# Six idle-time products on TensorE at the end of a gated scan, and GpSimd's splits of the second weight block behind a later wait

## The chip, the cores and the metric

The kernel runs on one core of one Trainium2 chip. Its time is the device time of one execution in microseconds (us). The core's engines are TensorE (PE in the rows; PEld is its weight load), VectorE (DVE), ScalarE (ACT), GpSimd (POOL) and SyncE (SP), which here only issues transfers. Each runs its own instructions in the order in which they are written, and they wait for one another through semaphores.

## The reference

Four layers stand in series, each added to its input and followed by a LayerNorm: an mLSTM attention layer, a mixture of 16 experts with the best 4 of each token, a gated linear attention (GLA) layer and a mixture of 32 experts with the best 8. There are 4 x 256 = 1024 tokens of 256 values in float32. The change lies between the end of the third layer and the start of the fourth:

```python
def step(S, inp):                      # GLA: 16 heads, 8 keys and 16 values each
    qt, kt, vt, gt = inp
    S = S * jnp.exp(gt)[..., None] + kt[..., None] * vt[..., None, :]
    ot = jnp.einsum('bhk,bhkv->bhv', qt, S)
    return (S, ot)
...
mu = o.mean(-1, keepdims=True)
var = ((o - mu) ** 2).mean(-1, keepdims=True)
o = (o - mu) * jax.lax.rsqrt(var + EPS)
o = o.transpose(0, 2, 1, 3).reshape(B, L, D)
return jax.nn.silu(gproj) * o @ Wo.T
...
logits = x @ gate_weight.T             # last layer: 32 experts
probs = jax.nn.softmax(logits.astype(jnp.float32), axis=-1).astype(logits.dtype)
topv, topi = jax.lax.top_k(probs, TOP_K)
...
gu = x @ w_gu.T
g, u = jnp.split(gu, 2, axis=-1)
h = jax.nn.silu(g) * u
acc = acc + h @ w_d.T * c_e[:, None]
```

## The kernel before, in words

**Precision.** Products of float32 values are done as three faster products: each operand is split into a rounded high part and the remainder, the low part, and `mm3` (its products are all put down to L1970) adds high x high, low x high and high x low. So each activation that goes into a product is first copied rounded out of PSUM by ScalarE (`XH`) and then subtracted by VectorE (`XL`); the latter counts up `lo_done` once for a pair of 128-token tiles. There are 8 tiles (`NT`), so each of the four LayerNorms' or head outputs' turnings brings `lo_done` up by 4: to 12 when the input of the GLA output projection is split (L1549), and to 16 when the input of the dense expert layer is (L1588). Weights are split by GpSimd: `high` (L811) rounds, `low` (L816) subtracts.

**The GLA scan.** The 16 value columns v are gone through one after another. TensorE's `spread(v)` (L2495) copies the values over the keys' rows, VectorE multiplies by the keys (L1904) and scans over the tokens (L1923), GpSimd multiplies the state by the queries (L824), and TensorE's `gather_o(v)` (L2507) sums over the keys with a 0/1 matrix of 32 columns. For the last v, GpSimd does half of the product (the 128x512 L824) and VectorE the other half. Between its steps GpSimd splits block 0 of the last layer's weights. ScalarE then copies and squares the outputs (L1251, L1252), TensorE sums the squares of each head (`sum_squares(k)`, L2547, once for each half of the values), VectorE makes the head's scale (L1355, L1356) and applies gate and scale (L1943, L1378) tile by tile, TensorE turns the tiles (L2225), ScalarE and VectorE split them, and TensorE does the output projection.

**The LayerNorm by halves.** `layernorm_by_halves` does tiles 0 to 3, then 4 to 7. VectorE takes the statistics (L1559, L1567), adds the small constant (L1569, 128x4) and inverts (L1570); ScalarE takes the root (L1010), VectorE makes the bias (L1576), and both normalise two tiles each (L1579, L1013). TensorE turns them (L2247), ScalarE makes the high part (L1019), VectorE the low part (L1588).

**The dense expert layer.** All 32 experts are computed for all tokens, in 8 blocks ("quads") of 4 experts. A block has 6 steps: 2 halves of the tokens x 3 chunks of 128 hidden values, 48 steps in all. `gate_up(i)` is 12 products (step 0's are L2290 and L2295). ScalarE applies SiLU to the gate (L1047) and, in the first `AHEAD` = 6 steps, copies the up part (L1052), and GpSimd multiplies the two (L880, `mixed_pool`). From step 6 on VectorE does that product (L1677). ScalarE's SiLU of step i waits for the product of step i - 2, and TensorE's step i waits for SiLU and copy of step i - 2, whose PSUM bank it takes. The down products run `LAG` = 10 steps behind.

**The router** runs beside steps 0 to 5. TensorE makes the logits (`route_half`, L2256) and turns them (L2264); VectorE does the rest in one chain of some 30 small instructions, each waiting for the one before: L1607 to L1611, the exponential on ScalarE (L1034), the eight largest (L1614), the rules (L1616 to L1652), and the combine weights `CW` (L1654 to L1665). Behind step 5 TensorE turns `CW` (`turn_weights`, L2328); it waits for it there, and what is behind it on TensorE waits, too. The turned weights are spread over rows and multiplied into the hidden values by GpSimd (L889).

**GpSimd's order** around the change is: the query products of the scan, with block 0's splits between them; the four splits of block 1 (gate/up high 128x1536 and low, down high 128x768 and low), today behind `lo_done` of 12; the six products of L880; then the splits of the later blocks between the L889. SyncE's transfers of block 3 wait for the splits of block 1 (`gate_split`, `down_split`), and the combine weights' transfer stands behind them.

`keep_warm(n, b)` writes n products of a zero matrix, 128 rows x 512 columns in bf16, into PSUM bank b; nobody reads them. It is there already at two places, 18 at the start (bank 7) and 2 behind the output projection (bank 0).

Of the kernel before, what the change touches and what calls it, by code (L numbers as in the profile page):

```python
# [28 lines left out]
def build_kernel(nc, a, out):  # L29
# [3 lines left out]
    NT = T // P  # L33
# [11 lines left out]
    DV1 = D // NH1  # L45
# [17 lines left out]
    with ExitStack() as ctx:  # L63
# [3 lines left out]
        def sem(name):  # L67
            return ctx.enter_context(nc.semaphore(name))
# [3 lines left out]
        def bank(n):  # L72
            return PS[:, n, :]
# [265 lines left out]
        lo_done = sem("lo_done")  # L339
# [147 lines left out]
        def quad_slot(q):  # L487

            n, c = GCOLS, DCOLS  # L490
            if q % 2 == 0:
                return [flat(EG[:])[:, 0:n], EW4[:, 0:n], EW4[:, n:2 * n],
                        flat(ED[:])[:, 0:c], EW4[:, 2 * n:2 * n + c], EW4[:, 2 * n + c:2 * n + 2 * c]]
            return [FA[:, 0:n], RA[:, 0:n], RA[:, n:2 * n],
                    FA[:, GLA_WORDS:GLA_WORDS + c], RA[:, 2 * n:2 * n + c], flat(W1H[:])[:, 0:c]]
# [52 lines left out]
        def _(sp):  # L548
# [15 lines left out]
            def load_expert(e, par):  # L564

                land_g, _, _, land_d, _, _ = MOE.slot(par)
                sp.dma_start(land_g.rearrange("p (k c) -> p k c", k=KD),
                             a["gateup0"][bass.ds(e, 1)].rearrange("o (k p) i -> p (o k) i", p=P)
                             ).then_inc(ld_exp[par], 16)
                sp.dma_start(land_d.rearrange("p (c d) -> p c d", d=D),  # L570
                             a["down0"][bass.ds(e, 1)].rearrange("o (c p) d -> p (o c) d", p=MOE.IP)
                             ).then_inc(ld_exp[par], 16)
# [68 lines left out]
        def _(pool):  # L641
# [195 lines left out]
                    low(dl, d, dh, whole, d_rounded).then_inc(down_split, 1)  # L837

            g, gh, gl, d, dh, dl = quad_slot(1)
            pool.wait_ge(lo_done, 3 * (NT // 2))  # L840
            pool.wait_ge(gate_ld[1], 32 * KD)
            g_rounded = high(gh, g, whole)
            low(gl, g, gh, whole, g_rounded).then_inc(gate_split, 1)
# [4 lines left out]
            def next_split(i):  # L848

                at, j = divmod(i, 2 * CHUNKS)
                q = at + 1
                if 2 <= q < QUADS:
                    g, gh, gl, _, _, _ = quad_slot(q)
                    if j == 0:
                        pool.wait_ge(gate_up_mm, 2 * 2 * CHUNKS * (q - 1))
                        pool.wait_ge(gate_ld[q % 2], 32 * KD * (q // 2 + 1))
                        rounded["g0"] = high(gh, g, half(0))
                    if j == 2:
                        low(gl, g, gh, half(0), rounded["g0"])  # L860
                    if j == 3:
                        rounded["g1"] = high(gh, g, half(1))
                    if j == 4:
                        low(gl, g, gh, half(1), rounded["g1"]).then_inc(gate_split, 1)
                q = at - 1
                if 2 <= q < QUADS:
                    _, _, _, d, dh, dl = quad_slot(q)
                    if j == 0:
                        pool.wait_ge(dn_done, 2 * CHUNKS * (q - 1))
                        pool.wait_ge(down_ld[q % 2], 16 * (q // 2 + 1))  # L870
                        rounded["d"] = high(dh, d, whole)
                    if j == 1:
                        low(dl, d, dh, whole, rounded["d"]).then_inc(down_split, 1)

            rounded = {}
            for i in range(STEPS + LAG - 1):
# [5 lines left out]
                v = i - (LAG - 1)  # L882
# [1080 lines left out]
        def _(pe):  # L1963
# [25 lines left out]
            def keep_warm(n, b):  # L1989

                for _ in range(n):
                    pe.matmul(bank(b), zb[:, 0:P], zb[:], start=True, stop=True, skip_group_check=True)
# [275 lines left out]
            def residual(src, tiles=range(NT)):  # L2268

                for t in tiles:  # L2270
                    pe.matmul(bank(4 + t // 2)[:, (t % 2) * D:(t % 2 + 1) * D], ident[:], src[:, t, :],
                              start=(t % 2 == 0), stop=True, skip_group_check=True)
# [6 lines left out]
            def moe_pe():  # L2279

                def gate_up_first():

                    b = step_bank(0)
                    _, gh, gl, _, _, _ = quad_slot(0)
                    pe.wait_ge(gate_split, 1)
                    pe.wait_ge(hi_done, 3 * (NT // 2) + 2)
                    for up in range(2):
                        for k, (xh, _) in enumerate(xm(0)):
                            for j, g in enumerate((gh, gl)):
                                pe.matmul(bank(b + up), chunk_of(g, k, up, 0), xh, start=(k == 0 and j == 0), stop=False,  # L2290
                                          skip_group_check=True)
                    pe.wait_ge(lo_done, 3 * (NT // 2) + 2)
                    for up in range(2):
                        for k, (_, xl) in enumerate(xm(0)):
                            ins = pe.matmul(bank(b + up), chunk_of(gh, k, up, 0), xl, start=False, stop=(k == KD - 1),  # L2295
                                            skip_group_check=True)
                        ins.then_inc(gate_up_mm, 1)
# [190 lines left out]
            def spread(v):  # L2488

                s = v % 2  # L2490
                if v >= 2:
                    pe.wait_ge(s_done, v - 1)
                for hf in range(2):
                    for i, part in enumerate((VTH, VTL)):
                        ins = pe.matmul(bank(2 * s + hf), rep1[:, v % 8, :], part[:, v // 8, hf * BANK:(hf + 1) * BANK],  # L2495
                                        start=(i == 0), stop=(i == 1))
                ins.then_inc(vr_mm, 1)

            def gather_o(v):

                pe.wait_ge(qs_done, v + 1)
                if v == DV1 - 1:
                    pe.wait_ge(qs_last, 1)
                for hf in range(2):

                    q = (32 * ((v % 8) // 2) + 64 * hf) % P
                    ins = pe.matmul(bank(4 + 2 * (v // 8) + hf)[q:q + 32, :], block2[:, v % 2, :],  # L2507
                                    QS[:, v % 2, hf * BANK:(hf + 1) * BANK], start=(v % 2 == 0), stop=(v % 2 == 1))
                ins.then_inc(qs_used, 1)
# [14 lines left out]
            def output_gate(t):  # L2524

                p = t // 2
                if t == 0:
                    pe.wait_ge(vt_lo, 4)
                    pe.wait_ge(w_split, 5)
                if t % 2 == 0 and p >= 2:  # L2530
                    pe.wait_ge(og_silu, p - 1)
                b = bank(6 + p % 2)
                mm3(b[:, (t % 2) * D:(t % 2 + 1) * D], xs(t), ws(W1H, W1L, G1, D), t % 2 == 0, True)
                if t % 2:
                    for part in (BGH, BGL):
                        ins = pe.matmul(b, rep1[0:1, 0, 0:1].broadcast_to([1, P]),
                                        part.unsqueeze(1).broadcast_to([1, 2, D]), start=False, stop=True,
                                        skip_group_check=True)
                    ins.then_inc(og_mm, 1)

            def sum_squares(k):

                pe.wait_ge(osq_act, 2 + k)
                for t in range(NT):
                    if k == 1 and t == NT // 2:
                        pe.wait_ge(osq_dve, 1)
                    ins = pe.matmul(bank(5)[:, t * NH1:(t + 1) * NH1], OSQ[k][:, t * P:(t + 1) * P], head_sum,  # L2547
                                    start=(k == 0 and t == 0), stop=(k == 1), skip_group_check=True)
                if k == 1:
                    ins.then_inc(osq_sum, 1)  # L2550
# [6 lines left out]
            for v in range(DV1):  # L2557
                if v + 2 < DV1:
                    if v + 2 == DV1 // 2:
                        pe.wait_ge(vt_lo, 4)  # L2560
                    spread(v + 2)
                for t in gate_tiles.get(v, ()):
                    output_gate(t)
                if v == SQUARES_AT:
                    sum_squares(0)
                if v == SQUARES_AT + 1:
                    residual(XA, (0, 1))
                if v == DV1 // 2:
                    pe.wait_ge(og_silu, NT // 2)
                gather_o(v)  # L2570
            sum_squares(1)

            pe.wait_ge(ot_evac, 3)
# [106 lines left out]
```

## Time and profile before

| | |
|---|---|
| median of 3 executions | 591.24 us (590.7 to 593.32) |
| the profiled execution, its own time | 589.8 us |
| its span | 588.0 us |
| TensorE busy (matmul) | 523.6 us, 89% of the span |
| GpSimd busy | 348.8 us, 59% |
| VectorE busy | 327.0 us, 56% |
| ScalarE busy | 230.5 us, 39% |
| chain that ended last, by engine | PE 61%, DVE 14%, DMA 5%, issue 5%, POOL 4%, ACT 2% |

All positions are us from the start of the span. In a row of the timeline stand the start, the length, the engine, the line of the kernel, the operation, output<-input and how many instructions the row merges; brackets at its end tell for how long the engine had been idle and what released it.
### The profile page before, as it was taken

What the parts mean: (1) busy time and instruction counts of PE and PEld (TensorE: products, weight loads), DVE (VectorE), ACT (ScalarE), POOL (GpSimd) and SP (SyncE); (2) the same over time, 40 slices, a digit from 0 to 9 for tenths busy, and PEclk for the clock granted to TensorE, in tenths of its full rate; (3) what the DMA queues carried; (4) which work ended last, traced back from release to release, by engine and by line L of the source; (5) the groups of instructions that cost most, each with busy time, mean ns of one, the idle gap of its engine ahead of it and who ended that gap; (6) DMA issues with size and microseconds to landing.
All of it is one profiled execution on the core that took longest, in us unless ns stands there. A gap on an engine that the chain in (4) does not pass through costs nothing.

```text
span 588.0 us, 9553 instructions
## 1 busy us (share of the span) xinstructions
PE 523.6 (89%) x3033; PEld 426.0 (72%) x3035; DVE 327.0 (56%) x726; ACT 230.5 (39%) x539; POOL 348.8 (59%) x316
## 2 busy tenths in 40 slices
PE   7999986339998999988989768999999999999994
PEld 4766666329887989966645438778888888888884
DVE  4635688634666444435998958563333252433276
ACT  3555542315554766545502022663232323232334
POOL 3394012777998797671377824254947657698180
PEclk9979998759998999999989968899999999999999
DMA  8999983245675766543000050204234343144022
GB/s 249 365 386 386 349 296 132 101 137 173 201 245 175 208 188 180 172 124 107 1 1 1 0 161 3 80 10 141 74 107 121 114 143 99 36 135 140 5 72 71
DMA packets 72864, 83.69 MB, mean 142 GB/s; under 512 B 7617, under 2 KB 63698, under 8 KB 72818
## 3 DMA queue, kind: packets, MB, share of 16 engines
q1 hardware_dynamic: 33490, 38.90, 22.0%
q10 hardware_dynamic: 35968, 35.26, 17.9%
q0 software_dynamic: 3360, 8.93, 4.9%
q8 instruction: 26, 0.43, 0.3%
q14 instruction: 20, 0.16, 0.1%
HBM read 48.61 MB, written 34.47 MB: 141 GB/s over the span
## 4 chain that ended last, share of the span: by engine, by line
PE 61%; DVE 14%; DMA 5%; issue 5%; POOL 4%; ACT 2%; ACTq 0%; DVEq 0%; POOLq 0%
PE PS L1970 47%; DMA FA<-xg 4%; POOL xg L708 3%; DVE FA L1923 2%; DVE PS L1904 2%; PE PS L2376 2%; PE PS L2495 2%; PE PS L2045 1%; PE PS L2067 1%; PE PS L2400 1%; PE PS L2507 1%; DVE HC L1378 1%; DMA FA<-yg,tix 1%; POOL FA L783 1%; PE PS L2192 1%
## 5 line engine op out<-in xcount | busy, mean ns | idle before, releaser
L1970 PE MATMUL PS<-XH,EW 128*128 128x512 f32 x392 | 129.8, 395 | 0.2 <-DVE EW L1278 0.2
L1677 DVE TENSOR_TENSOR FA<-OGATE,PS 128x512 f32<-128x512 f32 x42 | 28.9, 688 | 108.8 <-ACT OGATE L1047 90.7
L1970 PEld LDWEIGHTS PS<-XH,EW 128*128 128x128 f32 x392 | 73.7, 188 | 16.3 <-DVE EW L1278 0.7
L1970 PE MATMUL PS<-EW,XH 128*128 (+2 forms) x252 | 77.0, 389 | 3.6 <-issue 2.2
L1047 ACT ACTIVATE OGATE<-PS 128x512 f32<-128x512 f32 x48 | 28.7, 599 | 124.1 <-PE PS L1970 124.1
L1970 PE MATMUL PS<-XL,EW 128*128 128x512 f32 x196 | 77.0, 393 | 0.0
L1970 PE MATMUL PS<-EW 128*128 128x256 f32 x288 | 63.2, 284 | 0.6 <-DVE W1L L1682 0.4
L824 POOL TENSOR_TENSOR FA<-FA,QT 128x1024 f32<-128x1024 f32 (+1 forms) x16 | 37.4, 2338 | 32.5 <-DVE FA L1923 32.5
L1970 PE MATMUL PS<-EW,W1L 128*128 128x256 f32 x192 | 54.3, 283 | 0.0
L1970 PEld LDWEIGHTS PS<-EW 128*128 128x128 f32 x288 | 49.1, 189 | 4.2 <-DVE W1L L1682 1.5
L1970 PEld LDWEIGHTS PS<-EW,XH 128*128 128x128 f32 x252 | 44.8, 198 | 8.3 <-issue 2.8
L1682 DVE TENSOR_TENSOR W1L<-FA,EW 128x512 fp32r<-128x512 f32 x48 | 46.6, 978 | 2.8 <-ACT EW L1070 2.8
L1970 PE MATMUL PS<-EW,XL 128*128 (+2 forms) x126 | 46.6, 370 | 0.0
L889 POOL TENSOR_TENSOR FA<-FA,HC 128x512 f32<-128x512 f32 x24 | 34.5, 1442 | 16.7 <-DMA HC<-cw_room 16.7
L708 POOL DMA_INDIRECT xg<-XB,tix x32 | 31.3, 978 | 19.4 <-DVE tix L1463 10.4
L889 POOL TENSOR_TENSOR FA<-FA,QT 128x512 f32<-128x512 f32 x24 | 34.2, 1433 | 14.2 <-DMA QT<-cw_room 14.2
L1970 PEld LDWEIGHTS PS<-XL,EW 128*128 128x128 f32 x196 | 37.0, 189 | 6.8
L1970 PE MATMUL PS<-EW,EHH 112*128 x188 | 40.2, 306 | 0.1
L1923 DVE TENSOR_TENSOR_SCAN FA<-FA,PS 128x1024 f32<-128x1024 f32 x16 | 36.6, 2286 | 0.5
L1782 DVE TENSOR_TENSOR XL<-PS,XH 128x256 fp32r<-128x256 f32 x47 | 19.9, 424 | 30.0 <-ACT XH L1114 29.7
L1793 DVE TENSOR_TENSOR SQ<-SIL,PS 128x224 f32<-128x224 f32 x47 | 18.2, 388 | 32.7 <-ACT SIL L1133 32.2
L1970 PEld LDWEIGHTS PS<-EW,W1L 128*128 128x128 f32 x192 | 36.3, 189 | 0.0
(395 smaller groups left out, 1210.7 us busy)
## 6 DMA issues: line engine op xcount, KB each, us to landing
xg<-EQ ACTq DMA_DIRECT2D x1, 16384.0 KB, 60.7
EG<-in_gateup SPq DMA_DIRECT2D x16, 448.0 KB, 4.0
yg<-EQ ACTq DMA_DIRECT2D x1, 6016.0 KB, 19.7
FA<-xg ACTq DMA_DIRECT2D x47, 128.0 KB, 2.2
yg<-FA ACTq DMA_DIRECT2D x47, 128.0 KB, 2.6
ED<-in_down SPq DMA_DIRECT2D x16, 224.0 KB, 4.5
EG<-in_gateup SPq DMA_DIRECT2D x16, 192.0 KB, 3.0
FA<-in_gateup SPq DMA_DIRECT2D x16, 192.0 KB, 3.2
```

The costliest lines, as they stand in the source:

```text
L708: pool.indirect_dma_start(out=xg, out_offset=bass.IndirectOffsetOnAxis(ap=slots[:, n:n + 1], axis=0), in_=XB[:, t, :], in_offset=None).the ...
L824: pool.tensor_tensor(QS[:, v % 2, c], STATE[:, v % 2, c], QT[:, c], ALU.mult).then_inc(qs_done, 1)
L889: pool.tensor_tensor(mixed[:, v % MIXED, :], mixed[:, v % MIXED, :], spread_w[v % SPREADS], ALU.mult).then_inc(weighted, 1)
L1047: act.activation(sil_t[:, i % 2, :], bank(b), ACT.Silu).then_inc(sil_done, 1)
L1677: dve.tensor_tensor(mixed[:, i % MIXED, :], sil_t[:, i % 2, :], bank(step_bank(i) + 1), ALU.mult).then_inc(mixed_dve, 1)
L1682: dve.tensor_tensor(h_lo[:, v % TURNED, :], mixed[:, v % MIXED, :], h_hi[:, v % TURNED, :].bitcast(F32), ALU.subtract).then_inc(h_lo_done, 1)
L1782: dve.tensor_tensor(XL[:, :, c], bank(2 + i % 2)[:, 0:D].rearrange("p (k c) -> p k c", k=KD), XH[:, :, c].bitcast(F32), ALU.subtract).then ...
L1793: dve.tensor_tensor(HH[:, i % 2, 0:I], SIL[:, i % 2, 0:I], bank(i % 2)[:, I:2 * I], ALU.mult).then_inc(sh_ready, 1)
L1904: dve.tensor_tensor(spread_v(v), KT, spread_v(v), ALU.mult).then_inc(d1_done, 1)
L1923: dve.tensor_tensor_scan(STATE[:, v % 2, :], DEC, spread_v(v), 0.0, ALU.mult, ALU.add).then_inc(s_done, 1)
L1970: ins = pe.matmul(o, l, r, start=start and i == 0, stop=stop and i == n - 1, skip_group_check=True)
L2376: ins = pe.transpose(bank(2 + i % 2)[:, k * P:(k + 1) * P], XG[:, i % 4, k * P:(k + 1) * P], ident[:])
```

## The change

On GpSimd, the splits of block 1 wait for `lo_done` of 16 in place of 12. On TensorE, four `keep_warm` products come ahead of the last gathering (v = 15) and two behind it, into bank 0, which the last even-numbered v has left.

```diff
@@ -837,7 +837,7 @@
                     low(dl, d, dh, whole, d_rounded).then_inc(down_split, 1)
 
             g, gh, gl, d, dh, dl = quad_slot(1)
-            pool.wait_ge(lo_done, 3 * (NT // 2))
+            pool.wait_ge(lo_done, 4 * (NT // 2))
             pool.wait_ge(gate_ld[1], 32 * KD)
             g_rounded = high(gh, g, whole)
             low(gl, g, gh, whole, g_rounded).then_inc(gate_split, 1)
@@ -2567,7 +2567,10 @@
                     residual(XA, (0, 1))
                 if v == DV1 // 2:
                     pe.wait_ge(og_silu, NT // 2)
+                if v == DV1 - 1:
+                    keep_warm(4, 0)
                 gather_o(v)
+            keep_warm(2, 0)
             sum_squares(1)
 
             pe.wait_ge(ot_evac, 3)
```

TensorE's instructions around the last gathering (L2507; FA holds the query products, block is the 0/1 matrix, zb the zero matrix), before against after, with the semaphores waited for:

```order
 L2507 MATMUL PS<-FA,block 32x512 [waits qs_done]
 L2507 MATMUL PS<-FA,block 32x512
+L1992 MATMUL PS<-zb 128x512 x4
 L2507 MATMUL PS<-FA,block 32x512 [waits qs_last,qs_done]
 L2507 MATMUL PS<-FA,block 32x512
+L1992 MATMUL PS<-zb 128x512 x2
 L2547 MATMUL PS<-sums,FA 128x16 [waits osq_act]
 L2547 MATMUL PS<-sums,FA 128x16 x3
 L2547 MATMUL PS<-sums,FA 128x16 [waits osq_dve]
```

The four stand ahead of the wait for the last query product, the two ahead of the wait for the squares. The wait that changes on GpSimd has the same semaphore and another number, so its order of instructions is the same before and after.

## Rows read from the trace of the kernel before

**Rows 1.** Stretches: length, busy time of each engine, PEclk, DMA share, GB/s.

```profile
342.92:356.57 13.65, 10.92 (x46) 9.19 (x47) 6.98 (x18) 4.00 (x7) 1.49 (x1) 0.50 0.57 173
...
370.22:373.64 3.42, 3.42 (x9) 2.63 (x8) 2.01 (x10) 2.13 (x4) 0.00 (x0) 0.50 0.40 125
```

**Rows 2.** Timeline of TensorE around the last gathering.

```profile
333.27 1.85 PE L2547 MATMUL PS<-sums,SQ 128*128 128x16 f32 x16
...
341.53 1.05 PE L2507 MATMUL PS<-FA,block 128*32 128x512 f32 x4 [2.37 <-POOL FA L824]
...
344.46 1.92 PE L2507 MATMUL PS<-FA,block 128*32 128x512 f32 x4 [1.88 <-POOL FA L824]
...
347.57 3.60 PE L2547 MATMUL PS<-sums,FA 128*128 128x16 f32 x16 [1.19 <-ACT FA L1252]
```

**Rows 3.** Timeline of GpSimd and VectorE in the LayerNorm.

```profile
360.89 1.48 POOL L811 TENSOR_SCALAR EW<-FA 128x1536 fp32r<-128x1536 f32 x1 [16.48 <-DVE XL L1549]
...
362.46 3.49 POOL L816 TENSOR_TENSOR EW<-FA,EW 128x1536 fp32r<-128x1536 f32 x1
...
363.88 2.09 DVE L1569 TENSOR_SCALAR rv<-mv 128x4 f32<-128x4 f32 x1
...
366.46 0.30 DVE L1576 SCALAR_TENSOR_TENSOR nb<-mv,rstd 128x4 f32<-128x4 f32 x1 [0.27 <-ACT rstd L1010]
...
366.83 1.81 POOL L816 TENSOR_TENSOR W1H<-FA,EW 128x768 fp32r<-128x768 f32 x1
...
370.84 0.17 DVE L1569 TENSOR_SCALAR rv<-mv 128x4 f32<-128x4 f32 x1
```

**Rows 4.** ScalarE and VectorE split the dense layer's input; chain of waits, TensorE.

```profile
374.75 1.09 ACT L1019 ACTIVATE XH<-PS 128x512 fp32r<-128x512 f32 x2 [0.52 <-PE PS L2247]
...
375.39 1.42 DVE L1588 TENSOR_TENSOR XL<-PS,XH 128x256 fp32r<-128x256 f32 x4 [2.82 <-ACT XH L1019]
...
392.91 7.20 PE PS L1970 x31
```

**Rows 5.** Timeline of VectorE in the router.

```profile
380.48 0.69 DVE L1607 TENSOR_REDUCE LG<-PS 128x256 f32<-128x512 f32 x1 [3.67 <-PE PS L2264]
...
381.66 0.84 DVE L1611 TENSOR_TENSOR LG<-LG,rsum 128x256 f32<-128x256 f32 x1
...
385.65 1.31 DVE L1637 TENSOR_TENSOR t<-t,rsum 128x64 f32<-128x64 f32 x1
...
387.50 0.88 DVE L1642 SCALAR_TENSOR_TENSOR rbest<-rsum,rbest 128x8 f32<-128x8 f32 x1
...
388.68 0.23 DVE L1645 SCALAR_TENSOR_TENSOR t<-t 128x64 f32<-128x64 f32 x1
...
389.50 0.16 DVE L1657 SCALAR_TENSOR_TENSOR rsum<-rv,rsum 128x8 f32<-128x8 f32 x1
...
391.39 0.42 DVE L1665 TENSOR_TENSOR CW<-CW,rsum 128x256 f32<-128x256 f32 x1
```

**Rows 6.** Timeline of GpSimd beside the router.

```profile
379.66 2.56 POOL L880 TENSOR_TENSOR FA<-OGATE 128x512 f32<-128x512 f32 x2 [11.01 <-ACT OGATE L1052]
...
385.58 1.29 POOL L880 TENSOR_TENSOR FA<-OGATE 128x512 f32<-128x512 f32 x1 [3.36 <-ACT OGATE L1052]
...
387.07 1.29 POOL L880 TENSOR_TENSOR FA<-OGATE 128x512 f32<-128x512 f32 x1 [0.21 <-ACT OGATE L1052]
```

**Rows 7.** Timeline of GpSimd and VectorE in the sparse layer.

```profile
160.27 0.94 POOL L750 TENSOR_SCALAR EW<-EG 128x896 fp32r<-128x896 f32 x1
...
160.32 0.93 DVE L1631 TENSOR_TENSOR t<-t,rsum 128x32 f32<-128x32 f32 x1
```

**Rows 8.** Stretches around an earlier gap (columns as in rows 1); timeline of TensorE.

```profile
295.13:298.55 3.42, 1.56 (x7) 0.21 (x5) 3.42 (x4) 0.00 (x0) 1.85 (x1) 1.00 0.00 0
...
298.55:301.96 3.41, 3.01 (x10) 2.63 (x11) 3.38 (x3) 0.00 (x0) 2.99 (x2) 0.50 0.00 0
...
391.87 1.05 PE L2328 MATMUL PS<-ident,CW 128*32 128x128 f32 x8
```

## The prediction

> **What bounds the kernel now.** I read the granted clock by stretch first, then the stretch around the last gathering on TensorE, then VectorE against GpSimd from 360 to 392 us, and last the chain of waits. The clock shows two low stretches here: half speed (1.2 of 2.4 GHz) from 342.92 to 356.57 us and again from 370.22 to 373.64 [rows 1]. Before the first fall TensorE had done one 1.05 us gathering and then waited for GpSimd [rows 2]. What it does at half speed is on the path: the last gathering takes 1.92 us where the one before it took 1.05, and the second sum of squares takes 3.60 us where the first took 1.85 [rows 2]. Behind them come VectorE's head statistics and gating, the output projection, the LayerNorm, and the dense expert layer, where products follow one another, 31 in 7.20 us or 0.232 us each, twelve to a step, 2.8 us [rows 4]. It has to stop once there: the turning of the combine weights (L2328, start 391.87) needs the router's result from VectorE, whose last instruction (L1665) ends at 391.81 [rows 5, 8]. Today the two arrive nearly together.
>
> **The six products.** Four stand between the gatherings of v = 14 and v = 15, where TensorE is idle for 1.88 us, two between the last gathering and the sum of squares, where it is idle for 1.19 us [rows 2]. A product of 512 columns takes 0.23 us at full clock [rows 4], which I double for half clock. Four are 0.9 to 1.9 us against 1.88 of idle time, two are 0.5 to 0.9 against 1.19. So they cost nothing themselves; without that cover they would cost at most 2.8 us. If they hold the clock, the last gathering gives back 1.92 - 1.05 = 0.87 us and the sum of squares 3.60 - 1.85 = 1.75, together **-2.6 us**. Bounds: 0 (the clock falls all the same) and -2.6; behind the sum the slow transposes lie beside VectorE's gating, so I count nothing for them. I take -2.6, since the idle time behind the gathering of v = 14 falls from 1.88 + 1.19 to about 1.7 us, in two pieces.
>
> **The wait on GpSimd, in the LayerNorm.** `lo_done` reaches 12 when VectorE has done the low parts for the output projection; GpSimd begins the second block's splits there, at 360.89 us [rows 3]. They hold VectorE up: the tiny L1569 (128x4) takes 2.09 us and ends at 365.97, just as GpSimd's L816 ends (362.46 + 3.49 = 365.95); its second instance, with GpSimd idle, takes 0.17. The next two-operand instruction, L1576 (0.30 us), ends with the next split, too, and may give back 0.15 more [rows 3]. With the splits gone from here that is 1.92 + 0.15 = **-2.1 us**, on the path, since TensorE stands still for the normalised tiles. Bounds: -1.9 and -2.1. The SyncE queue is not late for it: it loads block 3 after `gate_split` reaches 2, now some 11 us later, but still ahead of its next wait, the combine weights.
>
> **The wait on GpSimd, in the router.** This is where I think the gain goes. `lo_done` reaches 16 with the last L1588, which ends at 375.39 + 1.42 = 376.81 [rows 4]. After the change it ends some 5.2 us earlier, at 371.6: 2.6 + 2.1, and 0.5 more, if the second low stretch goes with the shorter gap (L1019 was held until 374.75 by TensorE's slow products [rows 4]). GpSimd's four splits fill 360.89 to 366.83 + 1.81 = 368.64, 7.75 us [rows 3], so they now run from 371.6 to 379.4. The six products of gate and up (L880) queued behind them take 1.29 us each. The first two ran at 379.66 to 382.22 [rows 6]; the first now runs at 379.4 as before, although all else is 5 us earlier. From there GpSimd is never idle for long: products at 379.4, 380.7, 382.2, 383.6, 385.0, with 0.2 us let in for VectorE between two of them. The last waits for TensorE: step 4 needs the SiLU of step 2, which waits for the first product (380.7 + 0.5), and steps 4 and 5 take 2 x 2.8 us, so to 386.8; its operand is copied by 387.3 and it ends at 388.5.
> VectorE's router starts with L1607, at 380.48 before [rows 5]; by 2.6 + 2.1 and 1.2 for the low clock stretch, it starts at 374.6. Its chain from L1607 to the end of L1665 is 11.33 us, of which 2.2 are waiting today: L1611 takes 0.84 where a like instruction (L1665) takes 0.42, L1637 1.31 where L1645 takes 0.23, L1642 0.88 [rows 5]. L1637 and L1642 end within 0.1 us of a GpSimd product's end (386.87 and 388.36) [rows 5, 6]. Now GpSimd runs all through it. L1611 waits for the long split (to 376.7), L1620 for the last one, and L1623, L1635, L1637, L1639, L1642 each for one of the products, about 1 us each. The sixth product then catches L1645 or L1657. From its end at 388.5 the rest is 391.81 - 388.68 = 3.1 us or 391.81 - 389.50 = 2.3 [rows 5], so the weights are ready at 390.8 to 391.6, against 391.81 before. I take 391.3, **-0.5 us for everything up to here**: 5.4 of the 5.9 us that the router starts earlier are waited away. Bounds: no waits beyond today's, 385.9; every one of eleven two-operand instructions caught by a product, 392.6.
> The rows show single waits with idle GpSimd around them; that VectorE loses a whole GpSimd instruction at each of its two-operand instructions is shown by L1631, too, 0.93 us for 128x32, ended as L750 ends (160.27 + 0.94) [rows 7]. The Trainium skill (SBUF — State Buffer, "Who interferes with whom") speaks against this change here: a VectorE instruction with two SBUF inputs shares a read port with GpSimd, and the second to issue is blocked for the whole of the first. By that rule the router's chain waits as above and the sum is my forecast; by today's rows alone, three waits in the chain, the sum would be the first rival. The trace agrees with the rule for L1637 (1.31 us) and does not show back-to-back products against a chain.
>
> **The clock behind the new gap.** TensorE would end step 5 at 386.8 and stand still until 391.3, 4.5 us. Before, there is no such gap. After 295.13 to 298.55, with 1.56 us of work in 3.42, the next stretch was granted 0.50 although TensorE was busy 3.01 us in it [rows 8]; in 370.22 to 373.64 a stretch full of products at half speed lost 1.7 us [rows 1]. So returning work loses 0 (the low stretch lies within the gap) to 1.7 us, or 2.5 if the rise is late; I take **+1.6**, near the row of 370.22, since TensorE's work behind the gap is all on the path.
>
> **Sum.** -0.5 + 1.6 = +1.1 us against the profiled execution's 589.8, that is 590.9. The median shown is 591.24, 1.4 above that execution, so I forecast **592.3 us**. A measurement here tells about 0.5% from no change, 3 us: below 588.3 is faster, above 594.2 slower.
>
> **Rivals.**
> 1. **The router isn't held up.** If VectorE gets its turn between the products at no cost, the weights are there at 385.9 and TensorE, which the first product of GpSimd still holds until step 5 ends at 386.8, turns them at once: 386.8 - 391.8 = -5.0 us, 586.2. For it: today's VectorE reductions and PSUM readers don't wait. Against it: L1637, L1642, L1569 and L1631 did [rows 3, 5, 7].
> 2. **Half of the waits.** Some router instructions slip between products, the weights come at (385.9 + 391.3) / 2 = 388.6, 3.2 us earlier than before, the gap is under 2 us and the clock holds: 588.0.
> 3. **Slower: the clock falls at the last gathering all the same.** Then -2.6 is lost, everything from the sum of squares on is 2.6 us later with the router's waits unchanged: +1.1 + 2.6 = +3.7, 594.9. It decides if four products don't suffice before 342.92: the fall came 0.34 us after the gathering's end (342.58) [rows 1, 2], so only that much of the new work lies ahead of it, if the chip decides at the same moment.
> 4. **The products don't do what they are for, and the wait does nothing either** (splits and products move, the clock too): within 1 us, 591.2.
>
> **How the numbers follow.** Forecast (589.5 to 593.8) 0.50; rival 1 0.10; rival 2 0.15, half of it under 588.3; rival 3 0.17, most of it above 594.2; rival 4 0.08. Faster by over 0.5%: 0.10 + 0.08 = 0.18, to which I add 0.02 for a forecast with less of a gap: 0.20. Slower by over 0.5%: 0.15 from rival 3 and 0.02 from the forecast with every wait at its upper bound: 0.17. The same: 0.63. The range reaches from a little under rival 2 to rival 3: 587.2 to 594.9; the forecast's own is 589.5 to 593.8.
>
> **What would show it.** Right: the last gathering near 1.05 us and the sum of squares near 1.85, the granted clock 1.00 there; L1569 0.17; the splits starting as the last L1588 ends; L1623 to L1642 near 1.2 us each, ending with an L880; TensorE idle 3 to 5 us in front of L2328, released by L1665, and the clock low behind it. Wrong: L2328 starting within 0.5 us of step 5's end (rival 1), or L2547 still at 3.6 us (rival 3).

## The result, and the profile after

The changed kernel takes 593.09 us (median of 20 executions, 587.08 to 599.46), the kernel before, measured beside it, 589.49 (20 executions, 584.18 to 596.59). The ratio is 1.0062, with an interval of 1.0038 to 1.0087: 0.6% slower, 2.2 to 5.1 us. Ratios, here and below, leave out executions more than 1.5% above the fastest of the same kernel. The level before is 1.75 us lower than in the first three executions, so the forecast of 592.3 lies closer to the measured time than its step of +1.1 us does to the measured +3.6.

In the profiled execution (span 592.8 us) the gathering of v = 14 starts at 344.58, 3.05 us later than before [rows 2]; nothing ahead of it was changed. So positions are compared from that start on: the turning of the combine weights (L2328) comes 50.30 us behind it, before 391.87 - 341.53 = 50.34. Up to there nothing is won. I call this distance M, the time from the start of L2328 to the end of the span R (before 588.0 - 391.87 = 196.1, after 592.8 - 394.88 = 197.9), and the two together L: 246.5 before, 248.2 after.

TensorE around the last gathering, in the timeline of the changed kernel:

```profile
344.58 1.05 PE L2507 MATMUL PS<-FA,block 128*32 128x512 f32 x4 [2.37 <-POOL FA L824]
345.79 0.81 PE L1992 MATMUL PS<-zb 128*128 128x512 bf16 x3 [0.16 <-issue]
347.51 1.05 PE L2507 MATMUL PS<-FA,block 128*32 128x512 f32 x4 [0.91 <-POOL FA L824]
348.50 0.60 PE L1992 MATMUL PS<-zb 128*128 128x512 bf16 x2
349.75 1.96 PE L2547 MATMUL PS<-sums,FA 128*128 128x16 f32 x16 [0.65 <-ACT FA L1252]
```

They answer to [rows 2]. The last gathering takes 1.05 in place of 1.92 us, the sum of squares 1.96 in place of 3.60, and the new products lie in the idle time. This part went as forecast: -2.5 us.

The granted clock in the same profile, by stretch (length, busy time of PE, PEld, DVE, ACT and POOL, PEclk, DMA share, GB/s), against [rows 1]:

```profile
342.00:357.00 15.00, 9.59 (x63) 6.02 (x62) 10.81 (x22) 5.16 (x9) 4.17 (x2) 1.00 0.54 159
357.00:361.00 4.00, 3.15 (x13) 2.60 (x13) 3.90 (x13) 1.23 (x3) 0.00 (x0) 0.57 0.00 1
361.00:394.90 33.90, 28.52 (x156) 22.53 (x156) 24.32 (x82) 18.73 (x35) 16.64 (x12) 1.00 0.12 36
394.90:398.80 3.90, 3.90 (x15) 3.04 (x16) 0.68 (x1) 0.59 (x1) 1.59 (x1) 0.56 0.14 33
```

The long low stretch has gone, but a short one stands at 357 to 361, on the way into the output projection, and one at 395 to 399, behind L2328. The low stretch in the dense layer's first step has gone, too.

GpSimd and VectorE in the LayerNorm and ahead of the router, against [rows 3, 4]:

```profile
365.44 0.17 DVE L1569 TENSOR_SCALAR rv<-mv 128x4 f32<-128x4 f32 x1
374.25 1.42 DVE L1588 TENSOR_TENSOR XL<-PS,XH 128x256 fp32r<-128x256 f32 x4 [2.18 <-ACT XH L1019]
375.76 1.48 POOL L811 TENSOR_SCALAR EW<-FA 128x1536 fp32r<-128x1536 f32 x1 [28.31 <-DVE XL L1588]
377.32 3.49 POOL L816 TENSOR_TENSOR EW<-FA,EW 128x1536 fp32r<-128x1536 f32 x1
380.78 1.01 POOL L811 TENSOR_SCALAR EW<-FA 128x768 fp32r<-128x768 f32 x1
381.87 1.84 POOL L816 TENSOR_TENSOR W1H<-FA,EW 128x768 fp32r<-128x768 f32 x1
383.67 3.90 POOL L880 TENSOR_TENSOR FA<-OGATE 128x512 f32<-128x512 f32 x3
387.77 1.29 POOL L880 TENSOR_TENSOR FA<-OGATE 128x512 f32<-128x512 f32 x1 [0.20 <-ACT OGATE L1052]
```

L1569 has its 0.17 us, and the splits start 0.1 us behind the last L1588. They fill GpSimd until 383.7, where the first products (L880) begin, three of them without a break.

VectorE's router in the same timeline, against [rows 5]:

```profile
378.94 0.69 DVE L1607 TENSOR_REDUCE LG<-PS 128x256 f32<-128x512 f32 x1 [3.27 <-PE PS L2264]
...
380.12 0.97 DVE L1611 TENSOR_TENSOR LG<-LG,rsum 128x256 f32<-128x256 f32 x1
...
383.03 0.70 DVE L1620 SCALAR_TENSOR_TENSOR rv<-rsum,rbest 128x8 f32<-128x8 f32 x1
...
384.00 1.03 DVE L1623 TENSOR_TENSOR t<-top,rsum 128x64 f32<-128x64 f32 x1
385.07 1.19 DVE L1635 TENSOR_TENSOR t<-t,alpha 128x64 f32<-128x64 f32 x1
386.30 0.22 DVE L1636 TENSOR_REDUCE rsum<-t 128x8 f32<-128x64 f32 x1
386.55 1.10 DVE L1637 TENSOR_TENSOR t<-t,rsum 128x64 f32<-128x64 f32 x1
...
389.65 1.26 DVE L1647 TENSOR_TENSOR t<-top,t 128x64 f32<-128x64 f32 x1
...
392.62 1.24 DVE L1663 SCALAR_TENSOR_TENSOR CW<-HC,PR 128x256 f32<-128x256 f32 x1
393.90 0.93 DVE L1665 TENSOR_TENSOR CW<-CW,rsum 128x256 f32<-128x256 f32 x1
```

The chain from L1607 to the end of L1665 takes 15.89 us against 11.33. Nine instructions wait now (L1642, at 0.89, is the ninth), all with two operands in SBUF; before it was three (L1611, L1637 and L1642). Between them L1636, a reduction, takes its 0.22 us with GpSimd busy. TensorE pays for it in front of L2328:

```profile
394.88 1.83 PE L2328 MATMUL PS<-ident,CW 128*32 128x128 f32 x8 [3.33 <-DVE CW L1665]
```

It stands still for 3.33 us, and L2328 takes 1.83 us at the low clock in place of 1.05.

### The profile page after: what moved, and what is told of

The parts are those of the page before. It is cut to its first block, busy times and chain, and to the rows that moved or that the text cites. A ratio compares the mean times of both kernels' runs of the same rounds, so it can differ in the third digit from the quotient of the medians.

```text
span 592.8 us, 9564 instructions
## 1 busy us (share of the span) xinstructions
PE 525.8 (89%) x3038; PEld 424.4 (72%) x3041; DVE 330.7 (56%) x726; ACT 230.2 (39%) x539; POOL 348.6 (59%) x316
## 4 chain that ended last, share of the span: by engine, by line
PE 60%; DVE 13%; POOL 6%; DMA 6%; issue 5%; ACT 2%; ACTq 0%; POOLq 0%; DVEq 0%
PE PS L1970 46%; DMA FA<-xg 3%; POOL xg L708 3%; DVE FA L1923 2%; POOL FA L783 2%; DMA FA<-yg,tix 2%; DVE PS L1904 2%; PE PS L2067 2%; PE PS L2045 2%; PE PS L2376 2%; PE PS L2495 1%; PE PS L2400 1%; PE PS L2507 1%; DVE HC L1378 1%; PE PS L2030 1%
## 5 line engine op out<-in xcount | busy, mean ns | idle before, releaser
L1970 PE MATMUL PS<-XH,EW 128*128 128x512 f32 x392 | 131.3, 398 | 1.2 <-ACT OGATE L1047 1.0
L1970 PEld LDWEIGHTS PS<-EW 128*128 128x128 f32 x288 | 49.3, 190 | 4.3 <-DVE W1L L1682 1.5
L1970 PE MATMUL PS<-EW,XL 128*128 (+2 forms) x126 | 46.6, 370 | 0.0
L811 POOL TENSOR_SCALAR EW<-FA 128x768 fp32r<-128x768 f32 (+1 forms) x11 | 11.2, 1027 | 51.2 <-DVE XL L1588 28.3
```

The lines of the kernel that those rows point to most:

```text
L1970: ins = pe.matmul(o, l, r, start=start and i == 0, stop=stop and i == n - 1, skip_group_check=True)
```

## The experiments

Three groups of four kernels ran, each beside the kernel before, whose medians were 630.06 us (17 executions), 630.75 (23) and 589.90 (29). In the profiles of the first two groups, from two different chips, the part ahead of the gathering of v = 14 takes 37 to 53 us longer than in the first profile of before. The third group ran on the chip of the second and does not show this, so it isn't the chip; what it is stays open. The four ratios of the first group rest on two executions of before (624.06 and 615.14 us) and stand above the ratios of the medians, so they decide nothing, and I read M, R and L from the profiles there.

| kernel | M | R | L | L1607 to L1665 | gap at L2328 |
|---|---|---|---|---|---|
| before | 50.3 | 196.1 | 246.5 | 11.3 | none |
| before_again | 49.3 | 196.2 | 245.4 | 11.3 | none |
| changed | 50.3 | 197.9 | 248.2 | 15.9 | 3.33 |
| after_again | 50.2 | 199.2 | 249.3 | 15.9 | 3.33 |
| wait_only | 51.8 | 198.0 | 249.8 | 15.9 | 3.34 |
| products_only | 46.8 | 196.4 | 243.2 | 11.3 | none |
| parted (three profiles) | 45.0, 45.8, 45.0 | 196.2, 196.4, 196.2 | 241.1, 242.2, 241.2 | 11.6 | 0.3 |
| parted_only | 46.6 | 196.4 | 243.0 | 11.6 | 0.33 |
| warm_gap | 49.3 | 196.2 | 245.5 | 15.9 | filled |
| no_splits | 45.6 | 196.4 | 242.0 | 11.3 | none |
| two_only | 49.3 | 199.1 | 248.4 | 15.9 | 3.34 |
| four_only | 49.3 | 197.9 | 247.2 | 15.9 | 3.33 |

The kernel before once more (before_again, no edit) had a median of 589.48 us against 589.90 (0.9999, 0.9964 to 1.0035). Expected were L of 245.5 to 247.5 us, a last gathering of 1.9 and a sum of squares of 3.0 to 3.6; they were 245.4, just under, 1.92 and 3.60.

**How M adds up.** The profiles of one placement of the splits differ by a few parts only, and M can be worked out from these: a last gathering at half speed adds 0.87 us (1.92 - 1.05), a sum of squares at half speed 1.64 (3.60 - 1.96). Products_only has neither, 46.77; with both added that is 49.28, and before_again has 49.26. The changed kernel without either is 49.28 (two_only, four_only, warm_gap); with the slow gathering it is 50.15, as after_again has, and with both 51.79, where wait_only has 51.82. The parted splits without either are 44.97; with the slow sum 46.61, and parted_only has 46.59; with the slow gathering 45.84, as parted_again has. So moving the splits costs 2.5 us of M, as much as the products win where the last gathering keeps the clock, and parting them wins 1.8. The first profile of before has 1.1 us more than before_again. Those come from its second low stretch, 370.22 to 373.64 [rows 1], which before_again doesn't have: there the clock is 1.00 from 363 us to L2328.

The sum of squares took 1.96 us in all ten profiles with products and 3.60 in all four without. The last gathering is another matter: it took 1.92 us in three of the ten (after_again, parted_again, no_splits), and 1.05 in parted_only, which has no products there.

**Each half alone.** The products without the new wait:

```diff
-            pool.wait_ge(lo_done, 4 * (NT // 2))
+            pool.wait_ge(lo_done, 3 * (NT // 2))
```

> The changed kernel with the splits' wait put back to lo_done of 12: the six products alone. Measure M is the time from the start of the gathering of v = 14 (L2507) to the start of the turning of the combine weights (L2328): 50.34 us in the profile before, 50.30 in the changed kernel. Theory (the products hold the clock and are worth 2.5 us; the router's waits come from the moved splits): last gathering 1.05 us, sum of squares near 1.9, L1569 still near 2.1, L1607 to the end of L1665 near 11.3 us, M 46.5 to 47.9, TensorE idle under 1 us at L2328, time 2.5 to 3.8 us under before (ratio 0.9935 to 0.9958). Rival (the clock falls elsewhere instead and takes the gain back): M 49.5 to 50.5, ratio 0.999 to 1.001.

Median 626.14 us against 630.06 (ratio 1.0125, 0.9989 to 1.0261). M is 46.77, L 2.2 to 3.3 us under the two profiles of before. L1569 still waits:

```profile
400.13 2.08 DVE L1569 TENSOR_SCALAR rv<-mv 128x4 f32<-128x4 f32 x1
```

The wait without the products, which is the kernel before with 4 in place of 3:

> The kernel before with the splits' wait at lo_done of 16, without the six products. Theory: L1569 0.17 us, L1607 to the end of L1665 15 to 16.5 us, TensorE idle 3 to 4.5 us in front of L2328 and the clock low behind it for up to 3.5 us; the last gathering 1.9 and the sum of squares 3.6 us; M 52.3 to 53.1, time 3.8 to 4.8 us over before (ratio 1.0065 to 1.008). Rival (the wait alone gains by the freed L1569, and the changed kernel lost its time elsewhere): M 48 to 49, ratio 0.996 to 0.999.

Median 632.26 (1.0241, 1.0088 to 1.0394). M is 51.82, half a microsecond under the expected range; the chain (15.9 us) and the gap are as expected.

```profile
384.86 3.60 PE L2547 MATMUL PS<-sums,FA 128*128 128x16 f32 x16 [1.19 <-ACT FA L1252]
...
430.64 1.05 PE L2328 MATMUL PS<-ident,CW 128*32 128x128 f32 x8 [3.34 <-DVE CW L1665]
```

The gap is the same 3.34 us, although the products are missing and everything ahead of it lies elsewhere: the wait makes the gap by itself. The wait is the half that costs, 3.3 to 4.4 us of L against the two profiles of before; the products gain.

**The gap filled.**

```diff
-                    pe.wait_ge(cw_step, CW_READY)
                     pe.wait_ge(sil_done, AHEAD - 1)
                     pe.wait_ge(up_copied, AHEAD - 1)
+                    keep_warm(14, 2)
+                    pe.wait_ge(cw_step, CW_READY)
```

> The changed kernel with 14 more of the unread bf16 products behind step 5 of the dense layer, in the gap in front of L2328. Theory (the low clock behind the gap costs 1.9 us): M 50.0 to 50.6 as in the changed kernel, L2328 near 1.05 us, granted clock 1.00 behind it, from the start of L2328 to the end of the span 196.1 us as in the profile before against 197.9 in the changed kernel; ratio to before 0.999 to 1.002. Rival (the gap's low stretch costs nothing that isn't hidden): 197.9 us stays, ratio 1.003 to 1.008.

Median 632.65 against 630.06 (1.0193, 1.007 to 1.0315), which tells nothing between the two theories; its profile does. R is 196.2 as before, against 197.9 with the gap:

```profile
443.00:447.00 4.00, 3.99 (x22) 3.33 (x23) 0.73 (x2) 1.19 (x2) 1.64 (x1) 1.00 0.15 33
```

The clock is 1.00 behind L2328, so the low stretch behind the gap costs 1.7 us. The splits, and with them the transfers of block 3, are as late here as in the changed kernel, so their lateness costs nothing. In after_again and two_only the low stretch is longer and costs 2.9 us; both profiles are of long executions, 645.99 and 642.85 us. In after_again:

```profile
444.57:451.04 6.47, 5.99 (x19) 4.59 (x20) 1.10 (x2) 1.18 (x2) 2.01 (x2) 0.51 0.13 27
```

M, 49.29, is 0.7 us under what I expected: no low stretch fell into it here. In time it isn't shown that filling the gap wins anything.

**The changed kernel once more.**

> The changed kernel once more, on the chip of this group. M (start of the gathering of v = 14 to start of L2328) 49.2 to 50.4 us, the part from there to the end of the span 197.5 to 198.1, L1607 to the end of L1665 15.5 to 16.2, gap in front of L2328 over 3 us: all as on the first chip, if these are the program's own and not the chip's. Rival: they differ by more than 1 us from profile to profile, and the sum over these parts says nothing.

Median 631.99 against 630.75 (1.0014, 0.9972 to 1.0057): in this group the changed kernel isn't shown to be slower. M and the chain repeat, R doesn't (199.2 for 197.5 to 198.1). And the clock fell in the midst of the four products:

```profile
395.88 1.47 PE L1992 MATMUL PS<-zb 128*128 128x512 bf16 x4
397.83 1.92 PE L2507 MATMUL PS<-FA,block 128*32 128x512 f32 x4 [0.48 <-POOL FA L824]
399.68 0.62 PE L1992 MATMUL PS<-zb 128*128 128x512 bf16 x2
400.93 1.96 PE L2547 MATMUL PS<-sums,FA 128*128 128x16 f32 x16 [0.63 <-ACT FA L1252]
```

It is back before the sum of squares. The products don't always keep the clock up; what the profiles show is that the low stretch behind them is short. A low stretch of about 4 us also lies 7 to 12 us behind the start of the gathering of v = 14 in eight of the ten profiles with products, where it adds nothing to M. In the first profile of the changed kernel it comes at 357 us, 12.4 behind, and adds 1.0 (50.30 against 49.28); warm_gap has none.

**Two or four of the six.** Each kernel is the changed one without the other `keep_warm`.

> The changed kernel without the four products ahead of the last gathering, the two behind it kept. Theory (the four keep the clock from falling behind the gathering of v = 14): last gathering 1.9 us, sum of squares 3.0 to 3.6, M 51.5 to 53. Rival (the two suffice): gathering 1.05 to 1.9 and sum of squares under 2.2, M 49 to 50.5.

> The changed kernel with the four products ahead of the last gathering and without the two behind it. Theory (what counts is that the clock is back, or has not fallen, when the sum of squares starts; the four alone do that): sum of squares under 2.1 us, gathering 1.05 or 1.92, M 49.2 to 50.6. Rival (the two are what brings the clock back): sum of squares 3.0 to 3.6, M 51 to 53.

Gathering 1.05 and sum of squares 1.96 us in both, M 49.27 and 49.28; as single executions they took 642.85 us (before 630.75 in its group) and 590.96 (before 589.90). For two_only that is the rival's reading, but one profile doesn't show that the two suffice: in it a low stretch had ended 9.5 us ahead of the gathering of v = 14, as in parted_only, whose last gathering takes 1.05 us without any product, so this may be luck. What each of the six is worth stays open.

**Without the splits.**

```diff
-            g_rounded = high(gh, g, whole)
-            low(gl, g, gh, whole, g_rounded).then_inc(gate_split, 1)
+            one = lambda w: w[:, 0:2]
+            g_rounded = high(gh, g, one)
+            low(gl, g, gh, one, g_rounded).then_inc(gate_split, 1)
...
-            d_rounded = high(dh, d, whole)
-            low(dl, d, dh, whole, d_rounded).then_inc(down_split, 1)
+            d_rounded = high(dh, d, one)
+            low(dl, d, dh, one, d_rounded).then_inc(down_split, 1)
```

> The changed kernel with the four splits of block 1 cut to 2 columns each, waits and counts unchanged: most of block 1's high and low parts isn't computed. Theory (the splits, which still run when the router starts, delay the products of GpSimd and by them the router and TensorE): first L880 soon after the SiLU of step 0, L1607 to the end of L1665 11.0 to 12.0 us, no gap over 1 us in front of L2328, M 44.5 to 46. Rival (L880's six products alone hold the router up as long): L1607 to L1665 14 us or more, M 48 or more.

One execution, 625.31 us. The timeline of GpSimd (lines behind the edit are 1 higher):

```profile
412.99 0.20 POOL L816 TENSOR_TENSOR W1H<-FA,EW 128x2 fp32r<-128x2 f32 x1
414.64 2.56 POOL L881 TENSOR_TENSOR FA<-OGATE 128x512 f32<-128x512 f32 x2 [1.46 <-ACT OGATE L1053]
420.56 1.29 POOL L881 TENSOR_TENSOR FA<-OGATE 128x512 f32<-128x512 f32 x1 [3.37 <-ACT OGATE L1053]
```

With the same wait and no work behind it, the products keep the breaks that they have in [rows 6], the chain is back at 11.33 us and the gap is gone. What held the router up is the splits' 7.8 us of GpSimd, directly and by pushing the products together.

**Parted splits.** The products stay, the splits begin early again, and the three behind the first wait until VectorE is past the instructions that stalled (L1569, L1576):

```diff
-            pool.wait_ge(lo_done, 4 * (NT // 2))
+            pool.wait_ge(lo_done, 3 * (NT // 2))
             pool.wait_ge(gate_ld[1], 32 * KD)
             g_rounded = high(gh, g, whole)
+            pool.wait_ge(ln_bias, LN_BASE[2] + 1)
             low(gl, g, gh, whole, g_rounded).then_inc(gate_split, 1)
+            pool.wait_ge(ln_bias, LN_BASE[2] + 2)
             pool.wait_ge(down_ld[1], 16)
```

> The changed kernel with the splits begun at lo_done of 12 again, but parted: the rounding of the gate block first, its long low part only after the bias of the first half's LayerNorm (ln_bias, L1576), the down block after that of the second half. Theory (what costs is only which VectorE instruction lies beside which split): L1569 0.17 us twice, the splits done before the first GpSimd product, L1607 to the end of L1665 11 to 12 us, no gap over 1 us in front of L2328, M 44.7 to 46.0, time 4.3 to 5.6 us under before (ratio 0.9905 to 0.993). Rival (the low parts then hold up the second half's instructions, L1569 and L1588, and the gain is given back): M 46.5 to 48, ratio 0.994 to 0.998.

> The parted splits once more, beside the changed kernel. M 44.5 to 45.5 and 196.0 to 196.4 us behind it as in its first run; time 1.2 to 1.5% under the changed kernel and 0.8 to 1.1% under the kernel before. Rival: the gain is the chip's of the first group, under 0.5%.

> The kernel with products and parted splits, a third time. M 44.7 to 46.0, 196.0 to 196.5 us behind it, L 241 to 242.3; time 0.7 to 1.0% under before. Rival: the median differs from before by less than 0.5%.

Medians 624.21 against 630.06 (1.0081, 0.9994 to 1.0169), 624.80 against 630.75 (0.9915, 0.9828 to 1.0001) and 585.30 against 589.90 (0.9938, 0.9905 to 0.9971): 4.6 to 6.0 us less. M of the second, 45.84, is over its range, since the last gathering took 1.92 us there; L1569 is 0.17 twice in all three. GpSimd in the third profile (lines behind the edit are 2 higher, so L1571 is L1569 and L1578 is L1576):

```profile
356.87 1.48 POOL L811 TENSOR_SCALAR EW<-FA 128x1536 fp32r<-128x1536 f32 x1 [13.97 <-DVE XL L1551]
360.80 3.46 POOL L816 TENSOR_TENSOR EW<-FA,EW 128x1536 fp32r<-128x1536 f32 x1 [2.45 <-DVE nb L1578]
365.72 0.83 POOL L811 TENSOR_SCALAR EW<-FA 128x768 fp32r<-128x768 f32 x1 [1.46 <-DVE nb L1578]
366.64 1.83 POOL L816 TENSOR_TENSOR W1H<-FA,EW 128x768 fp32r<-128x768 f32 x1
```

and VectorE beside it:

```profile
359.90 0.17 DVE L1571 TENSOR_SCALAR rv<-mv 128x4 f32<-128x4 f32 x1
```

The long split lies between the two halves' biases, the last ends at 368.5, well ahead of the router. Both stalls are avoided. By the interval of the third group this kernel is 0.3 to 1.0% faster than the one before; the second group's interval just reaches 1. Its median is the lowest in each of the three groups.

**The same without the products.**

> The kernel before with the parted splits and without the six products. Theory (parting is worth 1.9 us in the LayerNorm, the products 1 to 2.6, and the two add up): L (start of the gathering of v = 14 to the end of the span) 243.5 to 245.0, last gathering 1.9, sum of squares 3.0 to 3.6, L1569 0.17, time 1.9 to 2.5 us under before (ratio 0.996 to 0.997). Rival (only the splits mattered): L 241 to 242.5 as with the products.

Median 587.15 (0.9924, 0.9892 to 0.9957), last gathering 1.05 us, sum of squares 3.60:

```profile
343.95 1.05 PE L2509 MATMUL PS<-FA,block 128*32 128x512 f32 x4 [1.87 <-POOL FA L824]
346.19 3.60 PE L2549 MATMUL PS<-sums,FA 128*128 128x16 f32 x16 [1.19 <-ACT FA L1254]
```

L is 242.97, half a microsecond under the expected range and 0.8 to 1.9 over the three with products. The medians agree (1.85 us), but the ratios stand the other way round (0.9938 with products, 0.9924 without) and their intervals overlap: that the products add to the parting is shown by the profiles, not by the times.

## Why the prediction was right and where it was off

**The way was right.** The mechanism, the place where the gain goes and the sign of the first comparison held: the LayerNorm's stall went, the router's chain lengthened by 4.6 us, a gap opened in front of L2328, and the clock fell behind it.

**The size was not.** I forecast +1.1 us and held 0.63 for "the same"; measured is +3.6 (2.2 to 5.1), past my bound of 3 us, a case I gave 0.17. L says +1.7 to +3.9 from profile to profile, and after_again +0.1% (-0.3 to +0.6), so how much slower the kernel is stays uncertain. Term by term:

- **The products, -2.6.** Here they gave -2.5 at their place, but the clock fell again at 357, which took 1.0 back: the last L2225 took 1.09 us there against 0.63, and L2271 1.59 against 1.03. Comparing L with and without them: products_only -2.2 to -3.3 against before, the changed kernel -0.5 to -1.6 against wait_only, parted -0.8 to -1.9 against parted_only. I took the upper bound of the term; the mean of these seven differences is -1.7. This term was the most mis-sized.
- **The LayerNorm, -2.1.** L1569 went from 2.09 to 0.17 in each kernel that moved the long split away, L1576 from 0.30 to 0.16. I spoke of L1576 as the next two-operand instruction, but L1569 isn't one: its row reads one tile (rv<-mv), and it had the longest stall.
- **The router.** I had the splits begin 30.1 us behind the gathering of v = 14; they begin at 31.2 (375.76 - 344.58). I had L1607 at 33.1; it is at 34.4. Of the 5.9 us that I moved it ahead, 1.2 were for the low stretch at 370.22, which before_again doesn't have, so that part was there to be won in one of the two profiles of before only. The chain was forecast at 16.7 and is 15.9. L2328 was to start at 49.8 and starts at 50.3. The waits fell on the instructions that I named up to L1642, but for L1639 (0.23 us), and at the end on L1647, L1663 and L1665, since the last product came later, and the next block's split behind it.
- **The clock behind the gap, +1.6.** 1.7 us by warm_gap and four_only, 2.9 by the long executions of after_again and two_only. The gap was forecast at 4.5 and is 3.3, with another 1.0 us between steps 3 and 4.

With -1.7 for the first term and 1.7 for the last the sum is +2.1, just under the measured interval; with 2.9 for the last it is +3.3, inside it. **Rival 1** falls by the chain of 15.9 us in six profiles. **Rival 3** is half true: in after_again the clock did fall at the last gathering, but it was back before the sum of squares, so it cost 0.9 and not 2.6. **Rival 2** falls by the gap of 3.3 us, **rival 4** by the sum of squares and the router's chain. The absolute 592.3 is near 593.09 partly because the three executions on which it was built lie above the median of the twenty, which is luck.

## What to carry to other kernels

When background work on GpSimd is moved off one critical chain of VectorE, look for the next chain that it lands beside, and count there every instruction with two operands in SBUF: each can be held until the GpSimd instruction beside it ends, and the nine held here lost 0.5 to 1.0 us each. Look at small one-operand instructions on SBUF, too: L1569 lost 1.9. Place such work by semaphores of VectorE's own steps, between its chains, rather than simply later. And price a clock stretch by several profiles: work that fills one idle place moves the low stretch, and takes only part of it away.

## What the hardware showed that I had not expected

- Each stalled instruction ends with the GpSimd instruction beside it or up to 0.3 us behind, even at 128x8: nine of them, against three before, made 4.6 us more in one chain. The Trainium skill (SBUF — State Buffer, "Who interferes with whom") says that a VectorE instruction with two SBUF inputs contends with a GpSimd instruction that reads SBUF, and that reductions never contend on this chip; the trace agrees with both (L1635 1.19 us, L1636 0.22).
- The gap was 3.33 or 3.34 us in five profiles on two chips, whatever the clock had done ahead of it. With the splits cut to 2 columns it was gone.
- The same unread products kept the clock in one profile and let it fall in the midst of them in another, and the same gap was followed by a low stretch of 3.9 us or, in two long executions, of 6.5. What the low clock costs is a matter of the execution as much as of the program.
